# A mixed attention layer on one core: weighted values in 32x64 tiles, values by way of DRAM, x loaded two groups ahead, and the norms' work moved between engines

## The reference

```python
def _layer_norm(h, w, b):
    mu = jnp.mean(h, axis=-1, keepdims=True)
    var = jnp.var(h, axis=-1, keepdims=True)
    return (h - mu) * jax.lax.rsqrt(var + LN_EPS) * w + b
...
xn = ln(x, g_norm)
q = (xn @ Wq).reshape(b, n, HEADS, DIM_HEAD).transpose(0, 2, 1, 3)
kv = xn @ Wkv
...
q = l2norm(q) * q_scale
k = l2norm(k) * k_scale
sim = jnp.einsum('bhid,bjd->bhij', q, k) * SCALE
...
attn = jax.nn.softmax(sim, axis=-1)
out = jnp.einsum('bhij,bjd->bhid', attn, v)
out = out.transpose(0, 2, 1, 3).reshape(b, n, HEADS * DIM_HEAD)
return ln(out @ Wout, g_out)
...
x = x + _L0_attn_ref(_L0_cond_ref(x, ...), ...)
x = x + _L0_ffn_ref(_L0_cond2_ref(x, mask_BxS_bf1, ...), ...)
```

## Time and profile before

| what | us |
|---|---|
| median of three runs | 832.1 |
| the profiled execution | 828.2 |
| its span from first to last instruction | 826.5 |
| PE, DVE, ACT, POOL busy | 720.0, 575.9, 520.1, 356.9 |
| mean granted TensorE clock | 0.946 |

### The profile page before, as it was taken

How to read it: one execution, slowest core, us unless ns; L and a number is a source line. 1 busy time by engine, 2 the same in 40 slices (tenths; PEclk the granted TensorE clock), 3 DMA queues, 4 the chain that set the end, 5 groups by cost and what they waited for, 6 DMA issues and landing times. The chain is left out here.

```text
span 826.5 us, 18078 instructions
## 1 busy us (share of the span) xinstructions
PE 720.0 (87%) x6080; PEld 576.1 (70%) x6080; DVE 575.9 (70%) x1735; ACT 520.1 (63%) x1519; POOL 356.9 (43%) x395
## 2 busy tenths in 40 slices
...
DMA packets 47786, 27.31 MB, mean 33 GB/s; under 512 B 22592, under 2 KB 45264, under 8 KB 47312
## 3 DMA queue, kind: packets, MB, share of 16 engines
...
...
q10 hardware_dynamic: 304, 0.01, 0.0%
...
## 5 line engine op out<-in xcount | busy, mean ns | idle before, releaser
L701 POOL TENSOR_TENSOR sb_sm<-sb_sm,sb_rden 128x128 f32<-128x128 f32 (+3 forms) x128 | 97.1, 764 | 230.5 <-DVE sb_rden L1177 230.4
L800 ACT ACTIVATE sb_sm<-sb_sm,sb_nmx 128x65 f32<-128x65 f32 (+3 forms) x512 | 178.2, 352 | 16.5 <-DVE sb_nmx L1173 16.1
L1166 DVE SCALAR_TENSOR_TENSOR sb_sm<-ps_S,sb_rq,sb_biasm 128x65 f32<-128x65 f32 (+3 forms) x512 | 112.2, 292 | 9.6 <-PE ps_S L1416 8.0
L683 POOL TENSOR_TENSOR sb_rq<-sb_qss,sb_mhalf 128x16 f32<-128x16 f32 x32 | 93.6, 2947 | 53.9 <-DVE sb_qss L1150 53.9
L693 POOL TENSOR_TENSOR sb_biasm<-sb_bias,sb_maskn 128x128 f32<-128x128 f32 (+3 forms) x128 | 109.1, 871 | 15.9 <-DVE sb_sm L1166 11.8
L800 ACT ACTIVATION_READ_ACCUMULATOR sb_sm<-sb_sm,sb_nmx 128x1 f32 x512 | 96.6, 189 | 0.0
L1294 PE MATMUL ps_M<-sb_xh,sb_wguh 128*128 128x512 f32 x78 | 39.0, 500 | 58.8 <-DVE sb_xl L1050 57.0
L1440 PE MATMUL ps_S<-sb_pT,sb_vblk 64*128 64x128 f32 (+1 forms) x896 | 83.3, 329 | 6.5 <-DVE sb_pT L1189 6.1
L1440 PEld LDWEIGHTS ps_S<-sb_pT,sb_vblk 64*128 64x128 f32 x896 | 70.1, 188 | 25.3 <-issue 11.1
L1453 PEld LDWEIGHTS ps_z<-sb_wout,sb_oT 128*128 128x128 f32 x512 | 62.9, 192 | 9.5 <-issue 6.0
L1453 PE MATMUL ps_z<-sb_wout,sb_oT 128*128 128x128 f32 x512 | 67.4, 279 | 0.0
...
## 6 DMA issues: line engine op xcount, KB each, us to landing
...
sb_vblk<-sb_vs SPq DMA_DIRECT2D x128, 32.0 KB, 1.9
...
```

The source lines that it names most:

```text
L683: pool.tensor_tensor(rq[:, cut], qss[:, cut], mhalf[:], ALU.pow).then_inc(q_rnorm.sem, 1)
L701: pool.tensor_tensor(p, p, stat(rden, g, j).unsqueeze(2).broadcast_to([128, 4, wide - 1]), ALU.mult)\
L800: ins = act.activation(p[:, t], p[:, t], ACT.Exp, bias=least[:, t:t + 1], accum_out=total[:, t:t + 1])
L1166: ins = dve.scalar_tensor_tensor(scored(g, j)[:, t], bank(g, "sim", n, odd)[:, first:first + wide], rq[:, col:col + 1], masked_bias(j % 4) ...
```

## The change

- **Values.** `vblk` and its memset go. `store_values` (step vst) writes the values of a group to a DRAM tensor in two DMAs, `spread_values` (vb.0, vb.1) reads each half back with one DMA, repeated on all four partition groups of `vrep`.
- **Weighted values.** `pv` is one step for each sequence. It has 32 matmuls on tiles of 32 rows by 64 columns: for each distance i of the key blocks, four row groups and two column halves, in four S banks. `pT` becomes a ring of two for a whole sequence each, sorted by distance, so `p_turn` places its squares otherwise. `ot_copy` copies two banks of 256 columns in place of one of 512, and Wout's rows are ordered to match.
- **Loads.** xg, xs and the mask have steps of their own (lx, ls, lm) in stage W, two groups ahead.
- **Norms.** `ln_1` stays in its PSUM bank until x1 is written. `ln_2` and `keys_normed` are activations on ACT (steps ln2 and kd); POOL computes the shift, minus mean times root. `result` keeps its product in its bank.
- **Order.** All lists of `ORDER` are written anew.

The order of the steady iterations, of SP, and the bodies that changed:

```diff
     "pe steady": """
-        sim.0-1 exp.0-4 down.0 sim.2 zT.0 sim.3 qkv.0 l1.0 sim.4 l1.1 PV.0 l1.2-3 scores.0 PV.1 sim.5 l2.0-3
-        mix.0 z.0 l3.0-2 sim.6-7 xnT.0 l3.3 z.1 kv.0 q.0-1 PV.2-4 q.2-3 l4.0 q.4 z.2 PV.5 qs.0-3 PV.6-7 z.3
-        q.5-7 z.4 kT.0 qs.4-7 z.5-7
+        sim.0 exp.0-3 sim.1 exp.4 down.0 zT.0 sim.2-3 qkv.0 l1.0 sim.4 l1.1 sim.5 l1.2-3 scores.0 l2.0-3 mix.0
+        PV.0 l3.0-1 sim.6-7 l3.2 xnT.0 l3.3 z.0 kv.0 q.0 z.1 q.1 PV.1 l4.0 q.2 z.2 PV.2 q.3-4 qs.0-3 q.5-7 z.3
+        kT.0 qs.4-7 z.4 PV.3 z.5-7
...
     "act steady": """
-        xh.0 exp.0-4 ex.0-2 down.0 zT.0 ex.3 qkv.0 l1.0-1 h1.0-1 l1.2-3 h1.2 ex.4 h1.3 ex.5-6 PV.0 ex.7 l2.0-1
-        h2.0 l2.2 h2.1 l2.3 h2.2-3 ex.8-9 l3.0-1 PV.1 ex.10 xnT.0 l3.2-3 ex.11-12 q.0-1 ex.13 PV.2 q.2 PV.3
-        ex.14-15 q.3 PV.4 q.4-6 PV.5 q.7 kT.0 PV.6-7
+        xh.0 exp.0-2 ex.0 exp.3 ex.1 exp.4 ex.2 down.0 zT.0 ex.3 qkv.0 ex.4 l1.0-1 h1.0-1 l1.2-3 h1.2-3 ex.5-7
+        l2.0-1 h2.0-1 l2.2 h2.2 l2.3 h2.3 ex.8 PV.0 ex.9 PV.1 ex.10 l3.0 ln2.0 l3.1 xnT.0 l3.2-3 ex.11 q.0
+        ex.12-13 q.1 PV.2-3 ex.14-15 q.2 PV.4 q.3 kd.0 q.4-7 PV.5 kT.0 PV.6-7
...
     "dve steady": """
-        xl.0 ln3.0 sim.0 exp.0 max.0 exp.1-3 max.1 sim.1 exp.4 max.2 zT.0 inv.0-1 down.0 max.3 zl.0 sim.2 inv.2
+        xl.0 ln3.0 sim.0 exp.0 max.0 exp.1 max.1 exp.2-3 sim.1 exp.4 max.2 zT.0 inv.0-1 max.3 inv.2 down.0 zl.0
...
     "sp fill": """
-        vb.0 maskn.0 rw.0 hw.0 wr.0
+        hw.0 lx.0 ls.0 vst.0 vb.0 wr.0 vb.1 lm.0
     """,
     "sp start": """
-        maskn.0 rw.0 hw.1 vb.0 wb.0
+        hw.1 lx.0 ls.0 vst.0 wb.0 lm.0 vb.0-1
     """,
     "sp steady": """
-        rw.0 maskn.0 wb.0 l4.0 vb.0
+        lx.0 vst.0 lm.0 ls.0 l4.0 vb.0 wb.0 vb.1
...
     if step == "PV":
-        return "SS" if k % 2 == 0 else ""
+        return "SSSS"
...
+            def store_values(g, k):
                 sp.wait_ge(v_shifted.sem, v_shifted.at(g, 1))
-                if g == 0:
-                    sp.wait_ge(v_cleared, 1)
-                sp.wait_ge(pv_psum.sem, pv_psum.at(g, 0))
-                for i in range(4):
-                    for c in range(4):
-                        sp.dma_start(vblk[c * QW:(c + 1) * QW, :, i, c % 2 * DH:(c % 2 + 1) * DH], vs[i * QW:(i + 1) * QW])\
-                            .then_inc(v_spread.sem, 16)
+                for spread in v_spread:
+                    sp.wait_ge(spread.sem, spread.at(g, 0))
+                for half in range(2):
+                    sp.dma_start(values[half].rearrange("q i d -> i q d"), vs[:, 2 * half:2 * half + 2].rearrange("p b d -> p (b d)"))                        .then_inc(v_stored.sem, 16)
+
+            def spread_values(g, half):
+                sp.wait_ge(v_stored.sem, v_stored.at(g, 32))
+                sp.wait_ge(pv_psum.sem, pv_psum.at(g, 2 * half - 2))
+                src = bass.AP(tensor=values.tensor, offset=half * S * 2 * DH, ap=[[0, 4], [8 * DH, QW], [1, 8 * DH]])
+                sp.dma_start(vrep[:, half].rearrange("p i d -> p (i d)"), src).then_inc(v_spread[half].sem, 16)
...
+            def ln2(g, k):
+                pool.wait_ge(ln_var["x"].sem, ln_var["x"].at(g, 2))
+                pool.tensor_scalar(shift[:], mv[:, 1, :, 0], -1.0, 0.0, ALU.mult, ALU.add).then_inc(mean_turned.sem, 1)
+                ln2_rstd(g, k)
+                pool.wait_ge(mean_turned.sem, mean_turned.at(g, 1))
+                pool.wait_ge(ln_rstd["x"].sem, ln_rstd["x"].at(g, 2))
+                pool.tensor_tensor(shift[:], shift[:], rstd[:, 1], ALU.mult).then_inc(n2_shift.sem, 1)
...
+            def ln_2(g, k):
+                act.wait_ge(n2_shift.sem, n2_shift.at(g, 1))
...
+                for b in range(GB):
+                    ins = act.activation(n1[:, b], x1[:, g % 3, b], ACT.Identity, scale=rstd[:, 1, b:b + 1], bias=shift[:, b:b + 1])
+                ins.then_inc(n2_ready.sem, 1)
...
+                for b in range(GB):
+                    ins = act.activation(kd[:, b], kv[:, b, 0:DH].unsqueeze(1).broadcast_to([128, 2, DH]), ACT.Copy,
+                                         scale=rk[:, b:b + 1])
...
-                act.wait_ge(pv_psum.sem, pv_psum.at(g, n // 2 * 2 + 2))
+                act.wait_ge(pv_psum.sem, pv_psum.at(g, n // 2 + 1))
                 act.wait_ge(z_psum.sem, z_psum.at(g, n - 1))
-                act.activation(half, bank(g, "PV", n // 2 * 2, n % 2)[:].rearrange("p (i t q) -> p i t q", i=4, t=4),
-                               ACT.Identity, bias=nval).then_inc(ot_copied.sem, 1)
+                for c in (n % 2 * 2, n % 2 * 2 + 1):
+                    ins = act.activation(oT[:, c::4].rearrange("p m (i q) -> p i m q", i=4),
+                                         bank(g, "PV", n // 2, c)[:, 0:256].rearrange("p (i m q) -> p i m q", i=4, m=2),
+                                         ACT.Identity, bias=nval)
+                ins.then_inc(ot_copied.sem, 1)
...
-                norm(n1, bank(g, "mix", 0)[:].rearrange("p (b d) -> p b d", b=GB), 0, mixed)
+                mixture = bank(g, "mix", 0)[:].rearrange("p (b d) -> p b d", b=GB)
+                norm(mixture, mixture, 0, mixed)
                 dve.wait_ge(mixed.sem, mixed.at(g, 1))
-                dve.tensor_tensor(n1, n1, row4(lnw), ALU.mult).then_inc(own_x.sem, 1)
+                dve.tensor_tensor(mixture, mixture, row4(lnw), ALU.mult).then_inc(own_x.sem, 1)
...
-                dve.wait_ge(pv_psum.sem, pv_psum.at(g, n + 1 - RING))
+                dve.wait_ge(pv_psum.sem, pv_psum.at(g, k - 1))
...
+            def pv(g, k):
+                ps = [free(g, "PV", k, c, (v_spread[k // 2], 16), (p_turned, 4 * k + 4)) for c in range(4)]
+                buffer = pT[:, (g * GB + k) % 2].rearrange("p (u m n q) -> p u m n q", m=2, n=2, q=QW)
+                for i in range(4):
+                    units = slice(UNITS[i], UNITS[i] + 4 - i)
+                    for c in range(4):
+                        rows = slice(c * QW, (c + 1) * QW)
+                        for odd in range(2):
+                            ins = pe.matmul(ps[c][odd * DH:(odd + 1) * DH, i * 2 * QW:256], vrep[rows, k // 2, i, k % 2 * DH:k % 2 * DH + DH],
+                                            buffer[rows, units, :, odd], start=(i == 0), stop=(i == 3), skip_group_check=True)
                 ins.then_inc(pv_psum.sem, 1)
```

More of the change, by code:

```diff
@@ L113 @@
-        pb.3 exp.4 rt.6-7 down.0 rt.8 qkv.0 scores.0 mix.0 rt.9 ln1.0 pl.1-2 ln2.0 nk.1 xnT.0 q.0-1 kv.0 q.2-3
-        kT.0 vs.0 q.4-7 ssq.0 ssc.0 pl.3
+        cg.0 pb.0 rt.0 x0.0 pb.1 rt.1-4 rw.0 pb.2 wl.0 pb.3 rt.5 exp.0-3 rt.6 exp.4 pl.0 rt.7 down.0 rt.8 qkv.0
+        scores.0 nk.0 pl.1 mix.0 ln1.0 rt.9 nk.1 pl.2 maskn.0 xnT.0 pl.3 q.0 kv.0 q.1-3 vs.0 q.4-5 xl.0 q.6-7
+        ssq.0 ssc.0
     """,
     "dve start": """
-        rw.0 xl.0 sim.0 max.0 exp.0 sim.1 exp.1 max.1 exp.2 inv.0 pl.4 max.2-3 exp.3 inv.1-2 sim.2 tp.0 max.4
@@ L118 @@
-        inv.3 tp.1 exp.4 sim.3 max.5 down.0 inv.4 tp.2-3 max.6 sim.4 inv.5 tp.4 qkv.0 max.7 inv.6 scores.0 tp.5
-        max.8-9 inv.7 mix.0 sim.5 inv.8-9 ln1.0 tp.6 max.10-11 tp.7-8 ln2.0 sim.6 xnT.0 max.12 tp.9 max.13 sim.7
-        maskn.0 inv.10 q.0 inv.11 q.1 max.14-15 tp.10 inv.12-13 tp.11 q.2 kv.0 tp.12-13 inv.14-15 q.3 tp.14 q.4
-        tp.15 q.5 kT.0 vs.0 pl.5 ssq.0 ssc.0 q.6-7
+        rw.0 xl.0 pl.4 exp.0 sim.0 exp.1 max.0 exp.2 inv.0 max.1 exp.3 sim.1 exp.4 max.2 tp.0 inv.1 sim.2 max.3
@@ L122 @@
+        tp.1 down.0 max.4 sim.3 inv.2-3 max.5-6 tp.2 qkv.0 scores.0 inv.4 tp.3 max.7 tp.4 mix.0 sim.4 inv.5-6
+        ln1.0 inv.7 max.8 tp.5 max.9 sim.5 tp.6 inv.8 max.10-11 tp.7 xnT.0 sim.6 inv.9 kv.0 tp.8 max.12 inv.10
+        maskn.0 vs.0 inv.11 tp.9 max.13 tp.10 sim.7 inv.12 q.0 max.14-15 tp.11-12 inv.13-14 q.1-2 inv.15
+        tp.13-15 pl.5 q.3-6 ssq.0 ssc.0 q.7
     """,
     "dve steady": """
[L124 removed]
@@ L129 @@
+        sim.2 max.4 tp.0-1 qkv.0 sim.3 max.5 l1.0-1 max.6 h1.0-1 l1.2-3 inv.3 tp.2 h1.2-3 tp.3 max.7 inv.4 sim.4
+        inv.5 tp.4 scores.0 inv.6 tp.5 sim.5 max.8 h2.0-1 max.9 inv.7 h2.2 mix.0 max.10 h2.3 ln1.0 maskn.0
+        max.11 tp.6 inv.8 tp.7 sim.6 inv.9 xnT.0 tp.8-9 sim.7 max.12-13 kv.0 inv.10 max.14 q.0 tp.10 max.15
+        inv.11-13 q.1 tp.11-12 vs.0 inv.14 tp.13 l4.0 inv.15 q.2-5 tp.14 q.6-7 tp.15 ssq.0 ssc.0
     """,
     "dve seventh": """
-        xl.0 ln3.0 sim.0 exp.0-3 max.0 sim.1 max.1-3 exp.4 sim.2 zT.0 down.0 inv.0-1 zl.0 tp.0 max.4 inv.2 max.5
@@ L132 @@
-        tp.1 qkv.0 scores.0 inv.3 sim.3 max.6 l1.0 tp.2 l1.1 h1.0-1 l1.2 inv.4 max.7 l1.3 mix.0 tp.3 h1.2-3
-        ln1.0 inv.5 sim.4 inv.6 ln2.0 tp.4 max.8 h2.0 tp.5 xnT.0 inv.7 tp.6 max.9 sim.5 kv.0 tp.7 sim.6 max.10
-        inv.8 h2.1 inv.9 max.11-12 q.0-1 h2.2 inv.10 kT.0 h2.3 max.13 q.2 tp.8 maskn.0 tp.9 q.3 sim.7 q.4-5
-        tp.10 inv.11 max.14 tp.11 q.6 inv.12-13 max.15 inv.14 ssq.0 ssc.0 tp.12 inv.15 vs.0 tp.13-15 q.7
+        xl.0 ln3.0 sim.0 exp.0-1 max.0-1 sim.1 exp.2 max.2 exp.3 inv.0 max.3 exp.4 inv.1 sim.2 zT.0 max.4 inv.2
```

192 lines of the change are left out of this document (84 added, 108 removed).

## The result

The changed kernel takes 730.17 us (median of 4 runs, 729.64 to 730.72), beside 832.43 for the kernel before on the same chip: a ratio of 0.877, with a 95% interval of 0.875 to 0.879. The forecast was 733, with 714 to 768 about it. The profiled execution has a span of 728.6 against 826.5, so 97.9 us less where the sum of the stages said 98.7.

What follows compares the result with a forecast made beforehand. PE's work plus its stalls, mostly waits for xl, were taken to bound the kernel. Stage savings summed to -98.7 us: 729.5 for the profiled run, 733 us for the median, range 714 to 768.

Steps and rivals of the forecast that it cites:

- Early x: Group boundaries: loading xg two groups ahead removes PE's stalls for xl and the half-speed clock behind them, at most 72.2 us.
- Experts' weights: Their loads, now issued later, still arrive in time: 0; rival, 3 us late at five boundaries: 748 us, chance 0.07.
- Values through DRAM: SP's queue: 16 issues become 2 stores and 2 loads; nothing of it is on the path, 0.
- The tiles: PV in 32x64 tiles: 1.30 us a block against 2.58 for two before, 41 us off PE over 32.
- Rival (a): PV records start no closer than 25 ns, so a block takes 1.60 plus 0.15 us: 747 us, chance 0.12.
- The four banks: Each PV needs all four S banks; copies taken as covered; rival, 0.95 us wait at 32 PVs: 763 us, chance 0.15.
- New idle: PE in steady iterations: 2.2 us for boundary copies, scoring before exp.0 and the four banks; 0 to 5.
- Norms and keys: Second norm and keys move from DVE to ACT: DVE 68.5 to 64.2, ACT 61.9 to 63.7 us, hidden beside PE.
- Fill: Stage up to 84.8 us: earlier ln1, second norm on ACT and earlier exp.0 give -7, from -3 to -10.
- Last and drain: Final stage of 107.5 us: PV -4.7 and waits for ACT's tables -0.4, together -5.1.
- Start: Stage of 92.3 us after the fill: two stalls go, PV gives 5.1, it ends at 63; -29, from -24 to -33.

Runs made afterwards that it cites:

- e4: Kernel before the change with only xg, xs and the mask loaded two groups ahead, by steps of their own: 774.6 us.
- e1: Changed kernel with the load of xg issued last in an iteration, behind vb.1, and not first: 770.3 us.
- e3: Changed kernel with values spread by 16 SBUF-to-SBUF DMAs and x's load behind them: 807.8 us.
- e8: Changed kernel with the 8 loads of the experts' weights issued behind vb.1 in the steady iterations: 763.6 us.
- e2: Changed kernel with values spread by 16 SBUF-to-SBUF DMAs at vb.1's place, no DRAM tensor, x still early: 730.2 us.
- e9: Changed kernel with norms and keys on DVE and the old steady lists of PE, ACT, DVE and POOL, PV places adapted: 798.9 us.
- e7: Changed kernel with the second norm and the keys' scaling back on DVE, POOL's shift gone: 737.0 us.
- e12: Changed kernel with sim.5 before l2.0, bias-table turns (fl.0-2) before xnT and six warm products before lg.1: 727.3 us.

## Why the prediction was right, point by point

- **Early x, at most 72.2.** Right in cause and size: alone it gave 56 (e4), where this part of the sum with its new waits was some 60. That the new order isn't what removed x's stalls is shown by e1 and e3.
- **Experts' weights, 0, at most 3 at each boundary.** Right, with 1.2 to 3.9 us of cover at the five boundaries (e8). What the prediction missed is that in the old list of the start there was none (9.8 in e4), so the early load alone would have lost a sixth of its gain there.
- **Values through DRAM, 0.** Right, e2.
- **The tiles.** 1.30 taken for a block, 1.35 measured. The stream of 0.84 ns a column held: on one tile, the next pass starts 0.215 us behind the second one of 256 columns. The term, 41 us, was a little large: blocks of before were 1.30 and 1.28 where they stood apart but 2.39 where two followed each other, 2.50 in the mean of a steady iteration, so 4.6 and not 5.1 an iteration. Rival (a), 1.75 a block, is out: eight tiles start inside 0.06 us and 64 records take 1.35, 21 ns a record. The rule of the Trainium skill that the prediction weighed, "TensorE: Matmul & The Clock Gate", section "Wait — 56ns, not 53.3ns?", has at least some 25 ns from one start to the next; for different tiles the trace disagrees, by these numbers.
- **The four banks, counted as small new idle.** Right for this order: 1.5 us of waits for copies and 3.1 of PV's waits for the scores of a sim in the whole run, nearly all in the start. But the reason was wrong: I held it covered because PE has other work between two PVs. That work must not be a sim, and ACT's copies must stand ahead of the exps; e9 is 62 us slower with lists in which they don't. The cover was the lists, and I priced these at nothing.
- **New idle, 2.2 an iteration.** Wrong: 0.9 us of idle are left in all, of 7.9. I kept the 2.3 of small waits of before and added to them. They went (xnT for the second norm, PV for pT; e4 still has both, at 8.3 and 6.1 us, and so has e9), and no z or scoring came. As e7 shows, the new lists took them. Of the 3.6 us that this leaves over, 2.4 are given back: PE's busy time fell by 4.5 and not by the 6.9 forecast, 0.5 of that in the tiles and 1.9 in products that start a little later without a recorded wait, which nothing here explains. The steady iteration is 80.9 and not 82.1.
- **Norms and keys.** DVE was forecast at 64.2 and is at 65.8, ACT at 63.7 and is at 63.4. ACT's activations of 128 columns take 484 ns (norm) and 392 (keys) and not 293, which was the time of a plain copy without a column for scale or bias; the copies of 256 columns are as forecast, 468. DVE's 1.6 too much is in one group: four hAl of an iteration take 4.3 us and not 2.8 as before, since two of them now run into POOL's work (last section). "Hidden" was off by 0.8 us in each of five steady iterations, 1.8 in the fill and 0.8 in the start (e7).
- **Fill, -7.** -3.8, of which 1.4 are only the two sims that changed sides. The parts that the sum names (ln1 1 earlier, the second norm 1.2 for 2.8, exp.0 2 earlier) make 4.6; what was to bring 7 isn't said. "exp.0 some 2 earlier" failed: it starts at 31.0 in both kernels. Ahead of it PE works through the routing's records of 8 columns. Before, it had no wait there and the clock was 1.00 up to 24.8; after, it waits 3.87 us for the tokens' DMA and runs 17 us at the half level. e12, where six warm products fill that wait, has exp.0 at 26.5. xnT came 4.5 us earlier all the same (63.98 against 68.48), and 1.9 of that are lost at once: the bias table's products now stand behind it, at 0.50 from 63.98 to 69.30, so the next product is 2.6 earlier (68.17 against 70.76).
- **Last and drain, -5.1.** -2.5. PV gave 4.2; l4p.0 (a product of the feed-forward that is put off to this stage) waited 1.39 us for ACT and ran behind it for 3.4 us at 0.50, a stall and 1.7 us of clock that the sum didn't have:

```profile
636.01 4.21 PE L1496 MATMUL ps_M<-sb_w,sb_hA 128*128 128x128 f32 x21 [1.39 <-ACT sb_hA L885]
```

The clock of that stretch:

```profile
636.00:639.40 3.40, 3.39 (x16) 3.39 (x17) 3.26 (x9) 3.39 (x14) 2.17 (x3) 0.50 0.01 2
```

- **Start, 63.** 62.3, DVE at 55.9 of it against 55.4.

So the total is right to 0.4%, and that closely in part by luck: the fill and the last stage were forecast 5.8 us too good and the five steady iterations 4.4 too bad, for reasons that have nothing to do with each other. With one of the two errors alone it would have been 0.6 or 0.8% off.
